# Sums of own rows: 32 adjacency columns stationary in four strips of one bank, then transposed

## The chip, the cores and the metric

The kernel runs on one core of one Trainium2 chip. The metric is the device time of one execution in microseconds (us), and of the kernel before three runs are shown. The engines are TensorE (PE, with its weight loads as PEld), VectorE (DVE), ScalarE (ACT), GpSimd (POOL) and SyncE (SP), which here only issues DMAs. Each works through its own program in order and waits for the others at semaphores.

## The reference

16 graphs of 512 nodes with 128 features go through four layers in a row, each with a residual and a layer norm: a graph convolution with the full adjacency (L0), five small graph convolutions over fixed groups of the first 25 nodes (L1), an attention over the adjacency (L2), and a block of convolutions, a distance matrix and a gated unit (L3).

```python
x = _layernorm(x + _L0_gnn_ref(x, adj, L0_gnn_weight, L0_gnn_bias), axis=-1)
# L0: support = einsum('bni,io->bno', x, weight); out = einsum('bnm,bmo->bno', adj, support) + bias
x = _layernorm(x + _L1_gnn_ref(x, adj, ...), axis=-1)   # written only for nodes 0..24
x = _layernorm(x + _L2_gnn_ref(x, adj, ...), axis=-1)
x = _layernorm(x + _L3_gnn_ref(x, adj, ...), axis=-1)
```

What the change touches is this part of L0: for the graphs 1 to 15 the product of the first 25 rows of the adjacency with x, which is 25 x 512 times 512 x 128 a graph, is needed early, because L1 works on these nodes alone.

## The kernel before

The program has a prologue and a loop. The prologue handles graph 0 up to L2 and, for the graphs 1 to 15 together, L0 and L1 on their 25 first nodes, packed as three tiles (PT = 3) of five graphs (PJ = 5), so that a tile has R = 125 rows. It also loads all weights, transposes them on PE and splits them in a high and a low part. The loop then does one graph a turn, and nothing of the change stands in it.

The 25 rows of each adjacency come in `adjP`, the full x of a tile in `xt[t]` (1280 KB each, loaded by SP in `x_tile`). `transpose_rows(t)` (L851) turns the adjacency rows on PE, ACT's `copy_rows(t)` (L443) puts them in `aPT`. `own_sums(t, graphs)` (L874) multiplies, for each graph and each of four chunks of 128 source nodes, x as the stationary operand (128 columns) by 100 adjacency columns as the moving one, so that the sums come out transposed, with the features on the partitions. Of the 100 columns 25 belong to the graph. ACT's `copy_sums(t)` (L448, L450) picks these into `TTs`, and `own_outputs(t)` (L881) multiplies them by the L0 weight `w0`. A product in float32 is two records in the trace.

There are 15 x 4 = 60 such products. PE has them in pieces between other work in an order that is written by hand: graphs 0 to 3 and then 4 of tile 0 around the first part of graph 0 (L966, L974), one graph of tile 1 ahead of L998, and the other nine graphs behind the transposes `block_rows` (L865). Behind them stand `transpose_weights(-1)` (L917), `own_outputs`, and the second aggregation of graph 0 (L257, L258, L259).

ACT takes its program in order too: `copy_sums(1)`, then `round_weights(-1)` (L479, L480), which copies what L917 wrote, then `copy_sums(2)`, then the exponential L517 and the scaling of the x rows (L520). The input of L517 is a dot product on DVE (L621, released by `dv_f`). DVE continues with L771 and L776 behind L517, and PE's second aggregation waits for L776.

SP loads conv2's weights into the place of `xt[0]` (L376), so it waits until tile 0 has been used (`q_TT` at 1), and behind this in its program stand x and the adjacency of graph 1 (L377, L379). The banks: tile 0's sums use bank 4, tile 1's bank 7, tile 2's bank 0; L998 uses bank 4, and L917's first blocks bank 4 again.

## Time and profile before

| | |
|---|---|
| runs | 588.64, 587.37, 587.83 us; median 587.83 |
| profiled execution | 587.87 us, of which the span is 586.1 us |
| TensorE's granted clock, mean | 0.993 of full |
| busy in the span | PE 568.1, DVE 476.6, ACT 341.3, POOL 120.7 us |
| prologue | from 0 to about 74 us |

The span is the time from the first to the last instruction; what lies around it (1.8 us here) belongs to the execution and not to the program. "Busy" counts the time in which an engine has an instruction under way. A timeline row gives the start, the duration, the engine, the line, the tiles, the shape and the count of like instructions that follow each other, and in brackets the idle time ahead of it with what ended it. The records of PE overlap: the distance from start to start is less than the duration of one.

### The profile page before, as it was taken

The page shows a single profiled execution, that of the slowest core. Times are in us where ns is not written, and L with a number is a line of the kernel's source. Part 1 is how long each engine was busy: PE and PEld are TensorE (multiplying, and loading weights), DVE is VectorE, ACT ScalarE, POOL GpSimd, SP SyncE. Part 2 cuts the span into 40 slices and gives each one's busy share as a digit, 9 for nine tenths or more (in the row PEclk, how much of TensorE's full clock was granted, in tenths as well). Part 3 has the DMA queues.
Part 4 walks back from the last instruction along what each step waited for, and adds up shares of the span by engine and source line. Part 5 has one row for each costly group of instructions (what it writes and reads, how often), then busy time and mean ns, then how long its engine had stood idle before and what let it go on. Part 6 is the DMA issues. An engine that isn't in the chain of part 4 may idle for free.

```text
span 586.1 us, 11733 instructions
## 1 busy us (share of the span) xinstructions
PE 568.1 (97%) x3579; PEld 488.0 (83%) x3579; DVE 476.6 (81%) x1798; ACT 341.3 (58%) x716; POOL 120.7 (21%) x140
## 2 busy tenths in 40 slices
PE   7998999999999999999999999999999999999894
PEld 6896987878979797979888897979797988889684
DVE  4778868888888888888888888888888888888665
ACT  2306646557575656675665757566657566575442
POOL 3310130312213030212131221303021313122110
PEclk9999999999999999999999999999999999999998
DMA  8980032030120303030303012030303030000000
GB/s 187 292 289 2 2 115 82 2 110 1 39 71 1 107 0 108 0 108 0 108 0 95 13 29 79 0 108 0 108 0 108 0 108 1 20 2 19 1 19 18
DMA packets 33300, 34.46 MB, mean 59 GB/s; under 512 B 1663, under 2 KB 22531, under 8 KB 33146
## 3 DMA queue, kind: packets, MB, share of 16 engines
q1 hardware_dynamic: 32986, 34.01, 18.5%
q8 instruction: 13, 0.21, 0.1%
q10 hardware_dynamic: 288, 0.13, 0.1%
q14 instruction: 13, 0.11, 0.1%
HBM read 29.74 MB, written 4.39 MB: 58 GB/s over the span
## 4 chain that ended last, share of the span: by engine, by line
PE 85%; DVE 1%; ACT 0%; issue 0%; POOLq 0%; POOL 0%; DVEq 0%
PE bank L257 14%; PE bank L258 13%; PE bank L259 13%; PE bank L1760 9%; PE pair L257 6%; PE pair L259 6%; PE pair L258 6%; PE bank L1594 4%; PE bank L1605 3%; PE bank L1696 2%; PE pair L1752 2%; PE pair L1684 2%; PE bank L1659 1%; PE bank L1702 1%; PE pair L1711 1%
## 5 line engine op out<-in xcount | busy, mean ns | idle before, releaser
L1133 POOL TENSOR_TENSOR rs<-ve,neg_half 128x4 f32<-128x4 f32 (+1 forms) x60 | 57.2, 953 | 279.1 <-DVE ve L1322 246.3
L257 PE MATMUL bank<-cd_hi,w_hi 128*128 128x256 f32 x272 | 77.5, 285 | 0.0
L258 PE MATMUL bank<-cd_lo,w_hi 128*128 128x256 f32 x272 | 76.7, 282 | 0.0
L259 PE MATMUL bank<-cd_hi,w_lo 128*128 128x256 f32 x272 | 76.5, 281 | 0.0
L1760 PE MATMUL bank<-P,msg 128*128 128x512 f32 x128 | 57.6, 592 | 0.0
L257 PE MATMUL pair<-aT_hi,x_hi 128*128 128x512 f32 x128 | 52.5, 410 | 0.6 <-DVE x_lo L776 0.3
L257 PEld LDWEIGHTS bank<-cd_hi,w_hi 128*128 128x128 f32 x272 | 51.3, 189 | 1.6
L258 PEld LDWEIGHTS bank<-cd_lo,w_hi 128*128 128x128 f32 x272 | 51.4, 189 | 1.4
L259 PEld LDWEIGHTS bank<-cd_hi,w_lo 128*128 128x128 f32 x272 | 51.3, 189 | 0.0
L259 PE MATMUL pair<-aT_hi,x_lo 128*128 128x512 f32 x128 | 50.2, 392 | 0.0
L258 PE MATMUL pair<-aT_lo,x_hi 128*128 128x512 f32 x128 | 50.0, 391 | 0.0
L1354 DVE TENSOR_TENSOR P<-bank,aT 128x512 f32<-128x512 f32 x64 | 41.1, 685 | 9.2 <-ACT bank L1182 9.1
L1341 DVE TENSOR_TENSOR aT_lo<-bank,aT_hi 128x512 fp32r<-128x512 f32 x56 | 38.5, 687 | 8.0 <-ACT aT L1178 8.0
L1176 ACT ACTIVATE aT_hi<-bank 128x512 fp32r<-128x512 f32 x56 | 34.4, 614 | 16.5 <-PE bank L1594 16.5
L1760 PEld LDWEIGHTS bank<-P,msg 128*128 128x128 f32 x128 | 23.1, 190 | 23.0 <-issue 23.0
L257 PE MATMUL bank<-co_hi,w_hi 128*128 128x256 f32 x144 | 41.9, 291 | 0.0
L258 PE MATMUL bank<-co_lo,w_hi 128*128 128x256 f32 x144 | 40.4, 281 | 0.0
L259 PE MATMUL bank<-co_hi,w_lo 128*128 128x256 f32 x144 | 40.4, 280 | 0.0
L1143 POOL TENSOR_TENSOR x<-x_nat,bias 128x512 f32<-128x512 f32 x15 | 19.7, 1316 | 76.6 <-DVE x3T_lo L1429 76.6
L1178 ACT ACTIVATE aT<-bank 128x512 f32<-128x512 f32 x56 | 34.7, 620 | 0.0
L1182 ACT ACTIVATE bank<-bank 128x512 f32<-128x512 f32 x64 | 34.4, 574 | 0.0
L1594 PEld LDWEIGHTS bank<-ident,adj_nat 128*128 128x128 f32 x224 | 26.2, 141 | 9.4 <-issue 7.4
(363 smaller groups left out, 1540.0 us busy)
## 6 DMA issues: line engine op xcount, KB each, us to landing
adj_nat<-in_adj_dram SPq DMA_DIRECT2D x16, 1024.0 KB, 6.1
x_nat<-in_x_dram SPq DMA_DIRECT2D x16, 256.0 KB, 2.9
xt<-in_x_dram SPq DMA_DIRECT2D x3, 1280.0 KB, 11.8
out_dram<-y_out SPq DMA_DIRECT2D x15, 256.0 KB, 2.2
hw<-in_L_gnn_W_dram SPq DMA_DIRECT2D x2, 640.0 KB, 6.9
xt<-in_L_gnn_conv_w_dram SPq DMA_DIRECT2D x1, 1088.0 KB, 9.7
aT<-in_adj_dram SPq DMA_DIRECT2D x5, 96.0 KB
nat_ih<-in_L_gnn_w_ih_dram SPq DMA_DIRECT2D x1, 384.0 KB, 5.4
```

The costliest lines, as they stand in the source:

```text
L257: nc.tensor.matmul(o, lh, rh, start=start, stop=False)
L258: nc.tensor.matmul(o, lh, rl, start=False, stop=False)
L259: return nc.tensor.matmul(o, ll, rh, start=False, stop=stop)
L1133: g.tensor_tensor(rs[i][:, 0:n], ve[i][:, 0:n], neg_half[:, 0:n], ALU.pow).then_inc(po_rs[i], 1)
L1143: g.tensor_tensor(x1[:, :, :], x_nat[1 - par][:, :, :], bc(bias0[:, :], NC), ALU.add).then_inc(po_xb, 1)
L1176: s.activation(aT_hi[:, mc, :], AT_OF[mc][:, :], ACT.Identity)
L1178: s.activation(aT[par][:, mc, :], AT_OF[mc][:, :], ACT.Identity).then_inc(ac_aT[mc], 1)
L1182: s.activation(AT_BANK[mc % 2][:, :], AT_BANK[mc % 2][:, :], ACT.Exp, scale=2.0).then_inc(ac_E[mc], 1)
L1341: v.tensor_tensor(aT_lo[:, mc, :], AT_OF[mc][:, :], f(aT_hi[:, mc, :]), ALU.subtract).then_inc(dv_aTlo[mc], 1)
L1354: v.tensor_tensor(P[:, mc, :], AT_BANK[mc % 2][:, :], aT[par][:, mc, :], ALU.mult).then_inc(dv_P[mc], 1)
L1594: last = t_.transpose(AT_OF[mc][:, ch(c)], adj_nat[par][:, c, ch(mc)], ident[:, :])
L1760: last = t_.matmul(X_BANK[:, :], msg[:, ch(mc)], P[:, mc, :], start=(mc == 0), stop=(mc == NC - 1))
```

## The change

The roles of the operands are exchanged. Now 32 adjacency columns (25 of the graph and 7 that follow) are stationary and 128 features of x move, so a sum comes out with the nodes on the partitions. `own_sums(q)` handles four graphs: graph number `slot` of the four writes the output partitions 32 x slot to 32 x slot + 31 of bank 4 and the columns of group q, and the four graphs take turns within each chunk of source nodes. The fourth group has three graphs. When all four groups are done, ACT copies the bank to `NAT` (`copy_natural`, two instructions; `NAT` is the space of `agg_sb`), PE transposes it in four pieces into bank 0 (`transpose_sums`), and one ACT instruction picks the 25 columns of each graph into `TTs`. `aPT` has three buffers instead of two and 132 columns instead of 125 a chunk, of which POOL fills the last seven once. The conv2 weights now wait for the second group of four, L998 writes bank 7 in place of bank 4, and x3M lies at another address.

```diff
@@ -12,6 +12,8 @@
 PT, PJ = 3, 5
 NT = PT + 1
 R = PJ * NODES
+SLOT = 32
+RW = R - NODES + SLOT
 SUB = 15
 NU = R + (NG - 1) * PJ * SUB
 SPAN = [(g[0][0], g[-1][1]) for g in GROUPS]
...
@@ -140,8 +141,9 @@
         xt = [early(f"xt{i}", [128, PJ, NC, D]) for i in range(PT)]
         nat_c2 = xt[0][:, :, :, :].rearrange("p j c d -> p (j c d)")[:, 0:D * TAPS].rearrange("p (i k) -> p i k", k=TAPS)
         nat_sum = xt[1][:, :, :, :].rearrange("p j c d -> p (j c d)")[:, 0:D * ODD].rearrange("p (i k) -> p i k", k=ODD)
-        aPT = [early(f"aPT{i}", [128, NC, R]) for i in range(2)]
+        aPT = [early(f"aPT{i}", [128, NC, RW]) for i in range(PT)]
         TTs = early("TTs", [128, PT, R])
+        NAT = agg_sb
         xP = early("xP", [128, PT, D])
         x1P = early("x1P", [128, PT, D])
         A5 = early("A5", [128, NT, NG, R])
@@ -152,7 +154,7 @@
         red0 = early("red0", [128, D])
         hw1 = early("hw1", [128, NG, HID])
         hw2 = early("hw2", [128, NG, 2, D])
-        hT = [aPT[h][:, 0:PT, :] for h in range(2)]
+        hT = [aPT[h][:, :, :].rearrange("p c r -> p (c r)")[:, 0:PT * R].rearrange("p (t r) -> p t r", t=PT) for h in range(2)]
         S2 = early("S2", [128, PT, D])
         R2 = early("R2", [128, PT, D])
...
+        NAT_BANK, TT_BANK = bank[4], bank[0]
         LATE = [[], [2, 3], [4, 5], [6, 7], [8]]
         LATE_AT = [[2], [3], [], [], []]
 
...
                 sp.dma_start(nat_hh[:, :, :], a["L3_gnn_w_hh"].rearrange("(g o) k -> o g k", g=3)).then_inc(q_wt, 16)
-                sp.wait_ge(q_TT, 1)
+                sp.wait_ge(q_sums, 2)
...
                 last.then_inc(q_zero, 1)
+                for t in range(PT):
+                    last = g.memset(aPT[t][:, :, R:RW], 0.0)
+                last.then_inc(q_pad, 1)
                 pool.wait_ge(q_ident, 1)
...
@@ -438,17 +444,19 @@
                                   ).then_inc(q_cst, 16)
                 def copy_rows(t):
                     act.wait_ge(q_aP, t + 1)
-                    if t > 1:
-                        act.wait_ge(q_TT, t - 1)
-                    s.activation(aPT[t % 2][:, :, :], bank[4 if t == 0 else 7][:, 0:NC * R].rearrange(
+                    s.activation(aPT[t][:, :, 0:R], bank[4 if t == 0 else 7][:, 0:NC * R].rearrange(
                         "p (c r) -> p c r", c=NC), ACT.Identity).then_inc(q_aPT, 1)
 
-                def copy_sums(t):
-                    act.wait_ge(q_TT, t + 1)
-                    s.activation(TTs[:, t, 0:R - NODES].rearrange("p (j n) -> p j n", n=NODES),
-                                 TT_BANK[t][:, 0:(PJ - 1) * R].rearrange("p (j n) -> p j n", n=R)[:, :, 0:NODES], ACT.Identity)
-                    s.activation(TTs[:, t, R - NODES:R], TT_BANK[t][:, (PJ - 1) * R - NODES:(PJ - 1) * R], ACT.Identity
-                                 ).then_inc(q_TTs, 1)
+                def copy_natural():
+                    act.wait_ge(q_sums, 4)
+                    s.activation(NAT[:, 0:3 * 128], NAT_BANK[:, 0:3 * 128], ACT.Identity)
+                    s.activation(NAT[0:3 * SLOT, 3 * 128:N], NAT_BANK[0:3 * SLOT, 3 * 128:N], ACT.Identity).then_inc(q_sumsb, 1)
+
+                def copy_sums():
+                    act.wait_ge(q_TT, 1)
+                    s.activation(TTs[:, :, :].rearrange("p t (j n) -> p (t j) n", n=NODES),
+                                 TT_BANK[:, 0:SLOT * (B - 1)].rearrange("p (g n) -> p g n", n=SLOT)[:, :, 0:NODES],
+                                 ACT.Identity).then_inc(q_TTs, 1)
 
                 def copy_u(t):
                     act.wait_ge(q_U, t + 1)
...
                 s.activation(U0[:, 0:NG, :], bank[6][:, 0:R].rearrange("p (g n) -> p g n", g=NG), ACT.Identity).then_inc(q_U0s, 1)
-                copy_sums(0)
                 copy_rows(2)
                 act.wait_ge(q_fuse, 2)
                 s.activation(fw[:, 2, :], fw[:, 1, :], ACT.Exp).then_inc(q_fe, 1)
@@ -510,9 +517,9 @@
                 act.wait_ge(q_S0, 1)
                 s.activation(S0[0:NODES, 0:4, :], bank[5][0:NODES, :].rearrange("p (g d) -> p g d", g=4), ACT.Identity)
                 s.activation(S0[0:NODES, 4, :], bank[6][0:NODES, 0:D], ACT.Identity).then_inc(q_S0s, 1)
-                copy_sums(1)
+                copy_natural()
                 round_weights(-1)
-                copy_sums(2)
+                copy_sums()
                 act.wait_ge(dv_f, 1)
                 s.activation(pef[:, 1, :], ef[:, 1, :], ACT.Exp, bias=c12[:, 1:2]).then_inc(ac_pf, 1)
                 hold(act, ac_pf, 1)
...
-                    o = bank[4][0:NODES, ch(gi)] if gi < 4 else bank[6][0:NODES, 0:D]
+                    o = bank[7][0:NODES, ch(gi)] if gi < 4 else bank[6][0:NODES, 0:D]
...
@@ -865,19 +872,30 @@
                             last = t_.transpose(o, A5[0:R, t, gi, :], ident[0:R, 0:R])
                     last.then_inc(q_BT, 1)
 
-                def own_sums(t, graphs):
-                    pe.wait_ge(q_aPT, t + 1)
-                    pe.wait_ge(q_xr[t], 16)
-                    for j in graphs:
-                        for mc in range(NC):
-                            lo = 0 if j < PJ - 1 else NODES
-                            last = t_.matmul(TT_BANK[t][:, 100 * j:100 * (j + 1)], xt[t][:, j, mc, :],
-                                             aPT[t % 2][:, mc, lo:lo + 100], start=(mc == 0), stop=(mc == NC - 1))
-                    if PJ - 1 in graphs:
-                        last.then_inc(q_TT, 1)
+                def own_sums(q):
+                    graphs = range(4 * q, min(4 * q + 4, B - 1))
+                    pe.wait_ge(q_pad, 1)
+                    pe.wait_ge(q_aPT, graphs[-1] // PJ + 1)
+                    for t in range(graphs[0] // PJ, graphs[-1] // PJ + 1):
+                        pe.wait_ge(q_xr[t], 16)
+                    for mc in range(NC):
+                        for slot, k in enumerate(graphs):
+                            t, j = k // PJ, k % PJ
+                            last = t_.matmul(NAT_BANK[SLOT * slot:SLOT * (slot + 1), ch(q)],
+                                             aPT[t][:, mc, NODES * j:NODES * j + SLOT], xt[t][:, j, mc, :],
+                                             start=(mc == 0), stop=(mc == NC - 1))
+                    last.then_inc(q_sums, 1)
+
+                def transpose_sums():
+                    pe.wait_ge(q_nT, 2)
+                    for q in range(4):
+                        pe.wait_ge(q_sumsb, 1)
+                        rows_ = SLOT * min(4, B - 1 - 4 * q)
+                        last = t_.transpose(TT_BANK[:, 128 * q:128 * q + rows_], NAT[0:rows_, ch(q)], ident[0:rows_, 0:rows_])
+                    last.then_inc(q_TT, 1)
 
                 def own_outputs(t):
-                    pe.wait_ge(q_TTs, t + 1)
+                    pe.wait_ge(q_TTs, 1)
                     return t_.matmul(bank[7][0:R, ch(t)], TTs[:, t, :], w0[:, :], start=True, stop=True)
 
                 def hidden(gi):
@@ -953,19 +971,16 @@
                     last = t_.matmul(AG_BANK[:, ch(c)], agg_sb[:, ch(c)], w0[:, :], start=True, stop=True)
                 last.then_inc(pe_out0, 1)
                 block_rows(0)
-                own_sums(0, (0,))
                 pe.wait_ge(q_row, 16 * 14)
                 pe.wait_ge(q_aPT, 2)
                 t_.matmul(bank[7][:, 0:D], vrows[0:NROWS, :], ident[0:NROWS, :], start=True, stop=True).then_inc(q_cols, 1)
-                own_sums(0, (1,))
                 pe.wait_ge(q_colsb, 1)
                 transpose_rows(2)
-                own_sums(0, (2, 3))
+                own_sums(0)
                 pe.wait_ge(dv_x1, 1)
                 pe.wait_ge(q_nT, 1)
                 t_.matmul(bank[6][:, 0:R].rearrange("p (g n) -> p g n", g=NG), x1[0:NODES, 0, :], nadjT[0:NODES, 0, :, 0:NODES],
                           start=True, stop=True).then_inc(q_U0, 1)
-                own_sums(0, (4,))
                 pe.wait_ge(q_zero, 2)
                 pe.wait_ge(q_U0s, 1)
                 pe.wait_ge(q_h1, 16)
@@ -990,23 +1005,22 @@
                         last = t_.matmul(o, hT0[:, 2 * gi + h, :], hw2[:, gi, h, :], start=(h == 0), stop=(h == 1))
                 last.then_inc(q_S0, 1)
                 pe.wait_ge(q_c12, 1)
-                own_sums(1, (0,))
                 pe.wait_ge(q_S0s, 1)
-                pe.wait_ge(q_TTs, 1)
                 for gi in range(NG):
-                    o = bank[4][0:NODES, ch(gi)] if gi < 4 else bank[6][0:NODES, 0:D]
+                    o = bank[7][0:NODES, ch(gi)] if gi < 4 else bank[6][0:NODES, 0:D]
                     last = t_.matmul(o, nadjT[0:NODES, 0, gi, 0:NODES], S0[0:NODES, gi, :], start=True, stop=True)
                 last.then_inc(q_o0, 1)
                 block_rows(1)
+                own_sums(1)
                 block_rows(2)
                 block_rows(3)
-                own_sums(1, range(1, PJ))
-                pe.wait_ge(q_nT, 2)
-                own_sums(2, range(PJ))
-                pe.wait_ge(q_own, 5)
+                own_sums(2)
+                own_sums(3)
+                pe.wait_ge(q_sumsb, 1)
                 pe.wait_ge(q_sc1, 1)
                 transpose_weights(-1)
-                pe.wait_ge(q_TTs, 2)
+                transpose_sums()
+                pe.wait_ge(q_own, 5)
                 for t in range(PT):
                     last = own_outputs(t)
                 last.then_inc(q_o, 1)
```

PE, early in the prologue, before. L874 are the products of own rows, L851 the transposes of tile 2's adjacency rows, L966 and L974 the small convolutions of graph 0:

```order
L959 MATMUL bank<-ident,vrows 128x128
L874 MATMUL bank<-aPT,xt 128x100 x4
L851 MATMUL bank<-ident,aT 128x125 x4
L874 MATMUL bank<-aPT,xt 128x100 x8
L966 MATMUL pair<-nadjT,x 128x125
L874 MATMUL bank<-aPT,xt 128x100 x4
```

The same place after, where L884 are the products, L858 the transposes of adjacency rows, L976 the former L959, L982 the former L966:

```order
L976 MATMUL bank<-ident,vrows 128x128
L858 MATMUL bank<-ident,aT 128x125 x4
L884 MATMUL bank<-xt,aPT 32x128 x16
L982 MATMUL pair<-nadjT,x 128x125
L989 MATMUL bank<-U,hw 128x100 x10
```

The 20 products of tile 0 in four pieces have become 16 in one piece, ahead of L982.

PE from the second layer of graph 0 (L990) to the own outputs (L881), before:

```order
L990 MATMUL pair<-hw,hT 25x128 x10
L874 MATMUL bank<-aPT,xt 128x100 x4
L998 MATMUL bank<-prod,nadjT 25x128 x4
L998 MATMUL pair<-prod,nadjT 25x128
L865 MATMUL bank<-ident,A 125x125 x15
L874 MATMUL bank<-aPT,xt 128x100 x36
L917 MATMUL bank<-ident,nat_w 128x128
L917 MATMUL bank<-ident,nat_wm 128x128
L917 MATMUL bank<-ident,nat_ws 128x128
L881 MATMUL bank<-w,TTs 125x128 x3
```

The same place after; L1005 is the former L990, L1011 the former L998, L872 the former L865, L935 the former L917, L894 the new transposes and L899 the own outputs:

```order
L1011 MATMUL bank<-prod,nadjT 25x128 x4
L1011 MATMUL pair<-prod,nadjT 25x128
L872 MATMUL bank<-ident,A 125x125 x5
L884 MATMUL bank<-xt,aPT 32x128 x16
L872 MATMUL bank<-ident,A 125x125 x10
L884 MATMUL bank<-xt,aPT 32x128 x28
L935 MATMUL bank<-ident,nat_w 128x128
L935 MATMUL bank<-ident,nat_wm 128x128
L935 MATMUL bank<-ident,nat_ws 128x128
L894 MATMUL bank<-ident,agg_sb 128x128 x3
L894 MATMUL bank<-ident,agg_sb 128x96
L899 MATMUL bank<-w,TTs 125x128 x3
```

No product stands ahead of L1011 any more, 16 stand between the transposes L872, 28 behind them, and four transposes are new behind the weights.

ACT from the copy of v (L508) to the exponential L517, before:

```order
L508 ACTIVATE v<-bank 128x256
L511 ACTIVATE prod<-pair 25x512
L512 ACTIVATE prod<-pair 25x128
L448 ACTIVATE TTs<-bank 128x100
L450 ACTIVATE TTs<-bank 128x25
L479 ACTIVATE plainT<-bank 128x3
L480 ACTIVATE plainT<-bank 128x2x128
L448 ACTIVATE TTs<-bank 128x100
L450 ACTIVATE TTs<-bank 128x25
L517 ACTIVATE pef<-ef,c 128x4
```

The same place after, where L515 is the former L508, L452 and L453 the new copy of the bank, L457 the new pick, and L524 the former L517:

```order
L515 ACTIVATE v<-bank 128x256
L518 ACTIVATE prod<-pair 25x512
L519 ACTIVATE prod<-pair 25x128
L452 ACTIVATE agg_sb<-bank 128x384
L453 ACTIVATE agg_sb<-bank 96x128
L487 ACTIVATE plainT<-bank 128x3
L488 ACTIVATE plainT<-bank 128x2x128
L457 ACTIVATE TTs<-bank 128x375
L524 ACTIVATE pef<-ef,c 128x4
```

Of the copies L448 and L450 none is left, and ahead of L487 stands the copy of the whole bank.

## Rows read from the trace of the kernel before

**Rows 1.** Page, busy time, share and instructions of each engine, whole span.
```profile
PE 568.1 (97%) x3579; PEld 488.0 (83%) x3579; DVE 476.6 (81%) x1798; ACT 341.3 (58%) x716; POOL 120.7 (21%) x140
```

**Rows 2.** Waits, 17 to 47 us: who waited, for whom, us in total, times, longest.
```profile
ACT TTs L448 <- PE bank L874: 8.3, 2, 7.5
```

**Rows 3.** Timeline of PE, 31 to 49 us: start, us, line, tiles, shapes, idle before.
```profile
31.43 1.11 PE L874 MATMUL bank<-aPT,xt 128*128 128x100 f32 x8 [0.54 <-DMA xt<-in_x_dram]
32.47 1.05 PE L998 MATMUL bank<-prod,nadjT 25*25 25x128 f32 x8
...
33.67 1.90 PE L865 MATMUL bank<-ident,A 125*125 125x125 f32 x15
35.41 8.18 PE L874 MATMUL bank<-aPT,xt 128*128 128x100 f32 x72
43.42 0.27 PE L917 MATMUL bank<-ident,nat_w 128*128 128x128 f32 x1
...
45.90 0.47 PE L257 MATMUL pair<-aT_hi,x_hi 128*128 128x512 f32 x1 [0.30 <-DVE x_lo L776]
...
48.75 0.60 PE L924 MATMUL bank<-ident,adj_nat 128*128 128x128 f32 x4
```

**Rows 4.** Timeline of ACT, 31 to 45 us.
```profile
31.42 0.25 ACT L512 ACTIVATE prod<-pair 25x128 f32<-25x128 f32 x1
...
43.95 0.17 ACT L479 ACTIVATE plainT<-bank 128x3 f32<-128x3 f32 x1 [4.46 <-PE bank L917]
...
44.49 0.32 ACT L517 ACTIVATE pef<-ef,c 128x4 f32<-128x4 f32 x1
```

**Rows 5.** Timeline of DVE, 41 to 45 us.
```profile
41.48 0.08 DVE L621 DVE_READ_ACCUMULATOR2_ANT ef<- 128x1 f32 x1
44.91 0.17 DVE L771 CAST x_hi<-pef 128x4 fp32r<-128x4 f32 x1 [3.35 <-ACT pef L517]
```

**Rows 6.** Timeline of PE, 20 to 29 us.
```profile
20.08 0.48 PE L959 MATMUL bank<-ident,vrows 28*128 28x128 f32 x2
...
21.47 0.65 PE L851 MATMUL bank<-ident,aT 125*128 125x125 f32 x4
...
23.81 0.48 PE L966 MATMUL pair<-nadjT,x 25*128 25x125 f32 x2
...
25.20 2.40 PE L974 MATMUL bank<-U,hw 128*128 128x100 f32 x20
...
28.55 2.34 PE L990 MATMUL pair<-hw,hT 128*25 128x128 f32 x20 [0.48 <-issue]
```

**Rows 7.** Timeline of PE, one place of the loop, at 84.75 us.
```profile
84.75 0.39 PE L1711 MATMUL pair<-ident_r,G 128*64 128x128 f32 x4
```

**Rows 8.** Timeline of ACT at 58.63 us.
```profile
58.63 0.49 ACT L471 ACTIVATE S<-bank 125x384 f32<-125x384 f32 x1 [0.23 <-PE bank L903]
```

**Rows 9.** Timeline of SP's DMA issues, 19 to 34 us.
```profile
19.06 0.43 SPq L365 DMA_DIRECT2D hw<-in_L_gnn_W_dram  x1
19.53 4.96 SPq L343 DMA_DIRECT2D xt<-in_x_dram  x2
...
31.44 1.52 SPq L376 DMA_DIRECT2D xt<-in_L_gnn_conv_w_dram  x1
...
33.84 1.41 SPq L379 DMA_DIRECT2D adj_nat<-in_adj_dram  x1
```

**Rows 10.** Lines L365, L343 and L379: first and last issue, issue to landing.
```profile
DMA to landing us min/median/max: 8.9/8.9/8.9
...
L343 SPq DMA_DIRECT2D xt<-in_x_dram x3: 390/1375/3547, 10.9 to 20.9; - x3
...
DMA to landing us min/median/max: 7.5/11.8/14.3
...
DMA to landing us min/median/max: 10.7/10.7/10.7
```

**Rows 11.** DMA issues, whole span: name, count, size, median us to landing.
```profile
adj_nat<-in_adj_dram SPq DMA_DIRECT2D x16, 1024.0 KB, 6.1
```

9 lines of the change are left out of this document (4 added, 5 removed).

## Prediction

> **What bounds the kernel now.** I read the page first: TensorE (PE) is busy for 97% of the span [rows 1], so a microsecond that leaves PE's path in the prologue should leave the end. The change touches only the prologue (before about 74 us), so I took the list of waits for the stretch 17 to 47 us: ScalarE (ACT) waits 8.3 us for the products of L874, the sums of own rows, [rows 2], and VectorE (DVE) then waits 3.35 us for ACT's L517 [rows 5]. The reader is to see one chain there. PE's timeline [rows 3] has 72 records of L874 from 35.41 for 8.18 us with no idle time in them, and only then the weight transposes of L917 at 43.42. ACT takes its work in the order written, so L479 (43.95) and L517 (44.49) stand behind PE's L917 [rows 4], although the input of L517, the last dot product on DVE, was done at 41.48 + 0.08 = 41.56 [rows 5]. From L517 go DVE's L771 at 44.91 [rows 5] and the second aggregation, L257 at 45.90, 1.41 us behind L517, which ends where L924 begins, at 48.75 [rows 3]. So the sums of own rows are the bound from 35 to 43 us. What stands in line behind them: the dot product (41.56, at most 44.49 - 41.56 = 2.9 us to be had unless it too moves), then the weights, x rows and adjacency that SP loads.
>
> **Products.** Before there are 60 products, each written as two records (120 in all), with 128 stationary and 100 moving columns. 72 records in 8.18 us, the last one 0.27 long: (8.18 - 0.27) / 71 = 0.111 us a record, 0.223 a product [rows 3]. After there are again 60 products of two records, with 32 stationary and 128 moving columns. The nearest row is L990, 25 stationary and 128 moving columns: (2.34 - 0.27) / 19 = 0.109 a record, 0.218 a product [rows 6]. So narrower weights alone bring 2%. The whole gain hangs on whether products for different strips of 32 output partitions run beside one another; no row of before has this (L990 and L998 always write the first strip). Bounds of a product:
> - no overlap: 0.218;
> - full overlap of the four: eight records in 0.218, 0.055 a product. L1711 issues weight load and matmul pairs (0.39 - 0.22) / 3 = 0.057 apart [rows 7], so pairs of that pace are possible, and 0.055 to 0.114 stands for full overlap;
> - the value I take, 0.14: the two records of a product go to the same strip and stay 0.109 apart; only the next product's first record may start beside the second record of this one, some 0.03 behind it (half of the pace of L1711, my estimate).
>
> The Trainium skill (TensorEngine Tiling (Array Packing), Overview) gives column tiling at 32 columns or fewer "Up to 4×", and its Key Properties say that tiles load weights and multiply in parallel; by that alone a product would cost 0.055 and the time would be that of rival B. TensorE: Matmul & The Clock Gate (Part 3, Packing small matmuls) says that matmuls start and end strictly in program order; with the two records of one product on one strip that order gives 0.14 instead. No row of before shows either.
>
> **Early part.** The program is moved too, as the order shows: 20 products of tile 0 that stood between L959 and L974 become 16 behind L851. L851 starts at 21.47 now, behind L874's second piece; after, it waits for L959 (20.08) and ACT's copy of it, some 0.8 later, so it starts near 20.85 and ends near 21.4 [rows 6]. 16 products of 0.14 end at 23.6, L966 starts there (23.81 before); its ACT copy takes until about 24.4 as now, and no product stands between it and L974, which starts at 24.45 instead of 25.20. That gives DVE's chain 0.75 us, so the dot product is done at 40.8. L990 gains less: its weights hw2 land at 19.06 + 8.9 = 27.96 [rows 9, 10], so it starts at 28.05 instead of 28.55, and L998 starts when ACT's L512 is done, at 31.42 + 0.25 - 0.5 = 31.17 [rows 4], say 31.25, instead of 32.47, since no product of tile 1 (landing 19.53 + 11.8 = 31.33 [rows 9, 10]) stands ahead of it.
>
> **Middle part.** From L998 at 31.25: ten records of 0.109 to 32.35; five transposes of L865 at 0.11, to 32.9 (DVE's operands for them come 0.75 earlier too); 16 products, 2.24, to 35.15; ten transposes, 1.1, to 36.25; 28 products, 3.9, to 40.2 (tile 2 is issued at 20.9 and has landed at 20.9 + 14.3 = 35.2 [rows 10], no wait). I add 0.1 for the changes between the shapes: the products end at 40.3 where they ended at 43.42. That is 3.1 us less.
>
> **What is added behind them.** Before, L517 came 44.49 - 43.42 = 1.07 us behind the products. After, the first step is a copy: PE's last record takes 0.27 to end, ACT copies 128x384 (the like of L471, 0.49, the next instruction starting 0.1 earlier [rows 8]) and 96x128 (0.25, as L512 [rows 4]), which ends 0.95 behind the products. PE's three transposes of L917 wait for this, because they write the same bank; they take 0.22 + 0.27, ACT's L479 starts at 1.45 and L480 ends at 1.85; the four transposes of sums are done by then, the copy of 375 columns takes 0.48 with 0.1 overlapped, and L517 starts 2.25 behind the products: 40.3 + 2.25 = 42.55. The chain behind the products is 1.2 us longer than before. Behind the waiting copies on ACT stand L517 and the scaling of x rows, behind the waiting transposes on PE the own outputs and the second aggregation. 42.55 is above the dot product's 40.8, so ACT still decides. The own outputs (six records, 0.65) and L917's four (0.45) fill PE from 42.7 to 43.8; the aggregation starts at 42.55 + 1.41 = 43.96 instead of 45.90. **The gain is 1.9 us.**
>
> **Moved transfers.** SP issued conv2's weights at 31.44 and the second adjacency at 33.84 [rows 9]. The first now waits for the second group of products (35.15), because it overwrites tile 0, so both go some 3.8 us later, the adjacency at 37.65. In the steady part an adjacency lands 6.1 us behind its issue, here in the crowd it took 10.7 [rows 10, 11]: 43.75 to 48.35, and it is wanted at 43.96 + 2.85 = 46.8 (2.85 is 48.75 - 45.90 [rows 3]). The crowd (tile 2 and what follows it) is gone by 38, so I take 45 and no cost; if the cover is gone, up to 1.5 us. The three fills on GpSimd, the bank exchange 4 to 7 for L998 and the new place of x3M cost nothing: GpSimd is idle until a DMA lands then, bank 7 is free, and x3M is written only in the loop. The rest of the prologue hangs on the aggregation and moves with it.
>
> Sum against the profiled execution: span 586.1 - 1.9 = 584.2, with 1.8 around it 586.0; that run (587.87) is 0.04 above the median of the runs, so **585.9 us**.
>
> **Rivals.**
> - B, full overlap. Products at 0.06: the early group ends at 22.4, DVE's chain gains 1.9 (dot product at 39.7), the products end near 36.9 (tile 2 lands at 35.2, 28 products take 1.7), and L517 starts at the dot product, 39.75: 4.7 us less. The aggregation would end at 45.90 - 4.7 + 2.85 = 44.05, before an adjacency that can hardly land ahead of 44.7: 0.7 given back, 583.9. For it: four separate strips. Against: the pairs of records on one strip.
> - C, no overlap, the other side. One mechanism: each product waits for the one ahead as in L990, at 0.218. The early group ends at 24.9 and L966 behind it, DVE's chain and L990 are 0.55 late, L998 starts at 32.3, and 10 records, 15 transposes and 44 products (9.6) end at 44.65; the chain behind is 1.2 longer, so L517 comes at 46.9, 2.4 late: 590.3. It decides from about 0.18 a product on: there 44 x 0.043 more uses up the 1.9. For it: L990 shows that a narrow stationary operand gives nothing by itself [rows 6]. Against: here four strips are named in turn.
> - D, the second adjacency becomes the bound: overlap as forecast, but landing at 48.3 instead of 45: 1.5 lost, 587.4. For it: 10.7 us now. Against: fewer bytes are ahead of it.
>
> **Chances.** Forecast 0.50 (its own range 584.6 to 587.0, from 0.11 to 0.165 a product), B 0.17, C 0.23, D 0.10. The likeliest gives 585.9. The range 583.4 to 589.8 leaves out the far half of C and a small part of B. No change means within 0.2%, 1.2 us, about what a measurement of this kernel can tell: faster has the forecast but 0.05 of it and B, 0.62; same has 0.05 and most of D, 0.14; slower has C and a rest, 0.24.
>
> **What would show it.** In the profile after: the 120 product records, and their spacing (pairs 0.11 apart with a short gap to the next: forecast; all near 0.03: B; all 0.11: C); last product near 40.3; L517's successor near 42.55 with ACT waiting first for the products, then for L917; the aggregation near 43.96; no wait of PE for adjacency at 46.8. I am wrong if strips share the array less than the pairs allow, if switching between shapes costs more than 0.1 in all, or if a transfer is late.

## The result

The changed kernel takes 584.18 us (median of 17 runs, 580.93 to 587.54) against 587.37 us for the kernel before on the same chips (17 runs, 585.7 to 590.47): a ratio of 0.9937, 95% interval 0.9917 to 0.9957. By the ratio that is 3.7 us less, by the two medians 3.2. Forecast were 585.9 us and a gain of 1.9. The time lies in the stated range and the direction was right; the gain is about twice the forecast one, and nearest to the time was rival B (583.9). The profiled execution has a span of 582.4 us, 3.7 less than the 586.1 of before.

Each run also has TensorE's mean granted clock over its span, and the two kernels differ in it. For the kernel before it was 0.990 to 0.997 in the 71 runs made beside the experiments; in the 24 of the changed kernel (17 here, 7 of after_again) it was 0.980 to 0.996, and in 8 of them below 0.990. At an equal mean clock the kernels lie further apart: at 0.993 the mean is 587.3 us over 20 runs of before and 583.3 over 7 of the changed kernel, at 0.996 586.2 over 21 and 581.9 over 2. From this I estimate that the change is worth about 4 us at equal clock and that a lower clock gives some of it back; the runs are of several chips, so the figure is rough.

The page of the profile after: the first line answers to [rows 1], with 7.8 us less on PE; the second is the granted clock in 40 slices of 14.6 us, in tenths.

```profile
PE 560.3 (96%) x3583; PEld 479.4 (82%) x3583; DVE 476.7 (82%) x1798; ACT 341.6 (59%) x713; POOL 120.8 (21%) x143
...
PEclk9989999999999999999999999999999999999998
```

PE's timeline after, which answers to [rows 3, 6]. L884 are the products; L858, L976, L982, L989, L1011, L872, L935 and L942 the former L851, L959, L966, L974, L998, L865, L917 and L924:

```profile
20.16 0.48 PE L976 MATMUL bank<-ident,vrows 28*128 28x128 f32 x2
20.93 0.74 PE L858 MATMUL bank<-ident,aT 125*128 125x125 f32 x4 [0.28 <-ACT cols L506]
21.60 1.08 PE L884 MATMUL bank<-xt,aPT 128*32 128x128 f32 x32
23.39 0.48 PE L982 MATMUL pair<-nadjT,x 25*128 25x125 f32 x2 [0.71 <-DVE x L682]
24.29 2.44 PE L989 MATMUL bank<-U,hw 128*128 128x100 f32 x20 [0.41 <-issue]
...
31.02 1.03 PE L1011 MATMUL bank<-prod,nadjT 25*25 25x128 f32 x8 [0.93 <-ACT prod L519]
...
32.19 1.30 PE L872 MATMUL bank<-ident,A 125*125 125x125 f32 x5
33.43 1.93 PE L884 MATMUL bank<-xt,aPT 128*32 128x128 f32 x32
35.29 1.56 PE L872 MATMUL bank<-ident,A 125*125 125x125 f32 x10
36.78 1.95 PE L884 MATMUL bank<-xt,aPT 128*32 128x128 f32 x56
39.49 0.33 PE L935 MATMUL bank<-ident,nat_w 128*128 128x128 f32 x1 [0.76 <-ACT agg_sb L453]
...
39.88 0.57 PE L894 MATMUL bank<-ident,agg_sb 128*128 128x128 f32 x4
...
42.29 0.47 PE L260 MATMUL pair<-aT_hi,x_hi 128*128 128x512 f32 x1
...
45.13 0.60 PE L942 MATMUL bank<-ident,adj_nat 128*128 128x128 f32 x4
```

The reader is to see three things. The 32 records of the first group take 1.08 us: (1.08 - 0.27) / 31 = 0.026 a record, 0.052 a product, where before a product took 0.223. The last 56 took (1.95 - 0.27) / 55 = 0.031, 0.061 a product; 24 of them belong to the group of three graphs, which fills three strips only. The 32 records at 33.43 take 1.93, and the five transposes ahead of them 1.30 where they should take 4 x 0.116 + 0.27 = 0.74 ((1.90 - 0.27) / 14 = 0.116 from the 15 of [rows 3]). And the last products end at 36.78 + 1.95 = 38.73 instead of at 43.59, while L989 starts at 24.29 instead of at 25.20.

ACT and DVE after, which answer to [rows 4, 5]: L452 and L453 copy the bank, L487 is the former L479, L457 picks the sums, L524 is the former L517; L628 is the end of the dot product, L778 the former L771.

```profile
38.79 0.49 ACT L452 ACTIVATE agg_sb<-bank 128x384 f32<-128x384 f32 x1 [7.92 <-PE bank L884]
39.17 0.26 ACT L453 ACTIVATE agg_sb<-bank 96x128 f32<-96x128 f32 x1
40.08 0.17 ACT L487 ACTIVATE plainT<-bank 128x3 f32<-128x3 f32 x1 [0.64 <-PE bank L935]
...
40.49 0.48 ACT L457 ACTIVATE TTs<-bank 128x375 f32<-128x375 f32 x1
40.90 0.30 ACT L524 ACTIVATE pef<-ef,c 128x4 f32<-128x4 f32 x1
```

```profile
40.78 0.08 DVE L628 DVE_READ_ACCUMULATOR2_ANT ef<- 128x1 f32 x1
41.29 0.17 DVE L778 CAST x_hi<-pef 128x4 fp32r<-128x4 f32 x1 [0.43 <-ACT pef L524]
```

L524 starts at 40.90, 3.59 us before the 44.49 of the kernel before, and the second aggregation at 42.29, 3.61 us before its 45.90; the span is 3.7 shorter. So in these two profiles the gain arose ahead of L524 and nothing of it was lost behind. The dot product ended at 40.78 + 0.08 = 40.86: DVE's wait for L524 fell from 3.35 to 0.43 us [rows 5]. Both inputs of L524 come at the same time here, the copy chain (L457 ends at 40.97, and the next instruction of ACT starts some 0.1 ahead of that end) and the dot product.

The granted clock in six microseconds of the prologue: stretch, its length, busy time and instructions by engine, the clock, DMA share and GB/s.

```profile
30.00:36.00 6.00, 5.07 (x52) 4.00 (x52) 5.93 (x23) 0.74 (x2) 0.00 (x0) 0.72 0.91 259
```

Half speed (1.2 GHz in place of 2.4) for about 3.4 of the six microseconds gives 0.72. That is what stretched L872 and the second group. There is another such stretch, from 11.9 to 15.3 us, in the first aggregation of graph 0, ahead of everything that was moved; I come back to it below.

### The profile page after: what moved, and what is told of

Its sections match the earlier page's. It is cut to its first block, busy times and chain, and to the rows that moved or that the text cites. A ratio compares the mean times of both kernels' runs of the same rounds, so it can differ in the third digit from the quotient of the medians.

```text
span 582.4 us, 11740 instructions
## 1 busy us (share of the span) xinstructions
PE 560.3 (96%) x3583; PEld 479.4 (82%) x3583; DVE 476.7 (82%) x1798; ACT 341.6 (59%) x713; POOL 120.8 (21%) x143
## 4 chain that ended last, share of the span: by engine, by line
PE 85%; DVE 1%; ACT 0%; issue 0%; POOLq 0%; POOL 0%; DVEq 0%
PE bank L260 14%; PE bank L262 14%; PE bank L261 13%; PE bank L1774 9%; PE pair L260 6%; PE pair L262 6%; PE pair L261 6%; PE bank L1608 4%; PE bank L1619 3%; PE bank L1710 2%; PE pair L1766 2%; PE pair L1698 2%; PE bank L1673 1%; PE bank L1716 1%; PE pair L1725 1%
```

## The experiments

| kernel | ratio to before, interval | median | products of the last groups | dot product ready | L524 starts | mean clock, 16 to 30 us | profiled run |
|---|---|---|---|---|---|---|---|
| before (profile) | | 587.37 | 8.18 | 41.56 | 44.49 | 1.00 | 587.87 |
| before, 2nd profile | | | 8.18 | 41.36 | 43.81 | 1.00 | 586.03 |
| after (profile) | 0.9937, 0.9917 to 0.9957 | 584.18 | 1.95 | 40.86 | 40.90 | 1.00 | 584.18 |
| after_again | 0.9951, 0.9923 to 0.9979 | 584.01 | 1.95 | 40.99 | 41.03 | 0.88 | 583.14 |
| slot_major | 0.9981, 0.9963 to 0.9999 | 586.37 | 3.86 | 41.81 | 45.23 | 0.88 | 587.61 |
| more_late | 0.9969, 0.9947 to 0.9990 | 585.42 | 3.69 | 42.23 | 44.10 | 0.76 | 587.42 |
| more_early | 0.9961, 0.9941 to 0.9981 | 585.21 | 1.95 | 41.54 | 41.58 | 1.00 | 584.85 |
| two_strips | one run | 584.68 | 2.48 | 41.34 | 41.38 | 1.00 | 584.68 |
| own_first | 0.9957, 0.9939 to 0.9974 | 584.45 | 1.99 | 41.56 | 41.66 | 0.76 | 584.08 |
| adj_first | 0.9950, 0.9929 to 0.9971 | 584.25 | 1.97 | 45.37 | 45.41 | 0.65 | 587.82 |
| pool_scale | 0.9958, 0.9936 to 0.9980 | 584.63 | 1.95 | 44.00 | 44.04 | 0.76 | 588.59 |
| warm | 0.9943, 0.9923 to 0.9962 | 582.21 | 1.95 | 39.56 | 39.60 | 1.00 | 581.70 |
| warm_best | 0.9934, 0.9921 to 0.9948 | 583.04 | 1.95 | 40.86 | 40.90 | 0.88 | 582.96 |

Times in us; the five columns on the right are of each kernel's one profiled execution, L524 under its name in the changed kernel (L517 before). The kernel before had medians of 587.07 beside after_again to more_early, 587.04 beside two_strips and own_first to pool_scale, and 586.68 beside the warm ones.

One reading goes for the whole table: the profiled run less the start of L524 is 542.1 to 543.4 us in twelve of the thirteen rows (pool_scale 544.6), while L524 itself moves by 5.8 us. So what tells the executions apart is almost all ahead of L524. And a profile need not be like the median of its kernel: those of adj_first, pool_scale and more_late were 3.6, 4.0 and 2.0 us above theirs, so that their L524 columns show a late execution, and where profile and median differ the verdict rests on the median.

**slot_major: the same products, strip after strip.**

```diff
-                    for mc in range(NC):
-                        for slot, k in enumerate(graphs):
+                    for slot, k in enumerate(graphs):
+                        for mc in range(NC):
```

> The order of the products is changed, graph by graph, so that the four chunks of one graph (one strip) follow each other and no two neighbours are in different strips except at the change of graph. All else as in the changed kernel. Theory 1 (the strips run beside one another, 0.027 us a record instead of 0.109): the records go back to 0.109 each, the products of the last two groups (56 records) take 6 us instead of 1.9, the last product ends near 43.5 and the time is 3 to 6 us above the changed kernel, so at or above the kernel before. Theory 2 (32 stationary columns are cheap by themselves, whatever the strip): same time as the changed kernel, within 1 us.

PE's timeline, the three groups of products, and ACT's exponential:

```profile
20.64 3.94 PE L884 MATMUL bank<-xt,aPT 128*32 128x128 f32 x32
...
33.99 4.05 PE L884 MATMUL bank<-xt,aPT 128*32 128x128 f32 x32
...
39.25 3.86 PE L884 MATMUL bank<-xt,aPT 128*32 128x128 f32 x56
```

```profile
45.23 0.29 ACT L524 ACTIVATE pef<-ef,c 128x4 f32<-128x4 f32 x1
```

The first two groups took longer for their 32 records than the third for its 56 because the clock was at half speed from 20.4 to 23.9 and from 34.1 to 37.5; only the third group is to be read for the pace. Nothing but the order was changed, and the median rose by 2.4 us (586.37 against 584.01 for after_again on the same chip; the two intervals just overlap, 0.9963 to 0.9979). L524 came 3.4 us behind the dot product, of which half speed in the second group explains about 1.7, an estimate from the 3.4 us at half speed. So the products bind again, and the records show that strips side by side are the source of their pace, not narrow weights: theory 1. But its sizes were off, in time (3 to 6 us) and in pace: 56 records took 3.86, (3.86 - 0.27) / 55 = 0.065 a record and not 0.109. The first half microsecond of this group and the next, in a windows view (instructions of PE and PEld in the second and third column):

```profile
39.24:39.70 0.47, 0.47 (x5) 0.46 (x5) 0.33 (x2) 0.00 (x0) 0.00 (x0) 1.00 0.55 94
39.70:40.17 0.47, 0.47 (x10) 0.47 (x9) 0.36 (x3) 0.00 (x0) 0.00 (x0) 1.00 0.42 150
```

Five records in the first 0.47 us, about 0.109 apart, ten in view in the next: I read this as the second strip's records starting while about half of the eight of the first strip still wait. Then twice as many run at once although the program gives them strip by strip. No record names its strip; the reading rests on the first five, which belong to one strip and stand 0.109 apart.

**two_strips: two strips in turns, then the other two.**

```diff
-                    for mc in range(NC):
-                        for slot, k in enumerate(graphs):
+                    for pair_ in (0, 2):
+                        for mc, slot in [(m, sl) for m in range(NC) for sl in (pair_, pair_ + 1) if sl < len(graphs)]:
```

> Within a group of four graphs the products of strips 0 and 1 take turns and are finished before those of strips 2 and 3. Theory 1 (a strip takes one record per 0.109 us, and records of different strips run beside one another if they are near in the program): two records run at a time, 32 records take about 1.9 us instead of 1.08, and the last 56 about 3.1 instead of 1.95, somewhat less where the next pair of strips starts beside the end of the first. Theory 2 (records are simply issued every 0.027 us on average, whatever the strip): 1.08 and 1.95 us as in the changed kernel.

```profile
22.18 1.54 PE L885 MATMUL bank<-xt,aPT 128*32 128x128 f32 x32
...
33.45 1.54 PE L885 MATMUL bank<-xt,aPT 128*32 128x128 f32 x32
...
36.20 2.48 PE L885 MATMUL bank<-xt,aPT 128*32 128x128 f32 x56
```

1.54 us for 32 records and 2.48 for 56, between the two theories: (1.54 - 0.27) / 31 = 0.041 a record, with four strips in turns 0.026, with one after the other 0.065. The order sets the pace by how many strips are near one another, and since two at a time would give 0.109 / 2 = 0.055 a record, more than two ran beside each other here too. L524 at 41.38 waited for the dot product, so in this single execution the products, at 0.082 each, no longer bound.

**more_late and more_early: the same extra work at two places.**

`signal` only keeps the repeated groups from raising the semaphore more than once; that part of the edit is left out here.

```diff
-                own_sums(2)
-                own_sums(3)
+                for signal in (False, True):
+                    own_sums(2, signal)
+                    own_sums(3, signal)
```

```diff
-                own_sums(0)
+                for signal in (False, False, True):
+                    own_sums(0, signal)
```

> The products of the third and fourth group are computed twice (56 records more, about 1.5 us of TensorE at full clock), behind the transposes of the adjacency blocks. Theory 1 (the bound is now the dot product on VectorE, ready at 40.84 where the exponential on ScalarE starts at 40.90, and TensorE has about 1.5 us to spare at full clock): the time rises by less than 1 us. Theory 2 (the products with the longer chain behind them still bound): the time rises by the full 1.5 us, and the exponential starts 1.5 us behind the dot product.

> The products of the first group are computed three times (64 records more, about 1.75 us of TensorE at full clock), ahead of the small convolution of graph 0 on which VectorE's chain hangs. Theory 1 (VectorE's chain, which starts from there, is the bound): the time rises by 1 to 1.75 us, more than in the run with the late products doubled, and the dot product is ready as much later. Theory 2 (only what stands at the late place counts): no change, within 0.5 us.

> The changed kernel once more, on the same chip as the others of this call: 0.993 to 0.995 of the kernel before. Theory on the clock: the granted clock fell to half for 3.4 us at 32 us in the profile of the changed kernel and not in that of before; if this belongs to the changed kernel, it is there again in this profile near that place; if it is chance, it is absent or elsewhere.

The repeated products in both:

```profile
38.27 3.69 PE L884 MATMUL bank<-xt,aPT 128*32 128x128 f32 x112
```

```profile
21.16 2.83 PE L884 MATMUL bank<-xt,aPT 128*32 128x128 f32 x96
...
46.37 0.66 PE L943 MATMUL bank<-ident,adj_nat 128*128 128x128 f32 x4 [0.39 <-DMA adj_nat<-in_adj_dram]
```

The extra work is 1.74 us (56 more records, 3.69 - 1.95) and 1.75 us (64 more, 2.83 - 1.08) in the profiles, the time rose by 1.4 and 1.2 us against after_again, and the intervals overlap, so the times don't tell the theories apart. The profiles say more. In more_late L524 came 1.87 behind the dot product: the spare time that theory 1 claimed was used up. The extra 1.74 is more than the 1.36 to spare in after_again (below), and half speed (21.0 to 27.9 and 34.7 to 38.1) had delayed PE as well. In more_early L524 followed the dot product at once (41.54, 41.58) although 64 records more stood ahead. Its last row also shows PE waiting 0.39 us for the second adjacency, which no other profile has. In after_again, where the clock was full behind 24.1 us, ACT waited 1.36 us for the dot product:

```profile
41.03 0.30 ACT L524 ACTIVATE pef<-ef,c 128x4 f32<-128x4 f32 x1 [1.36 <-DVE ef L628]
```

So with the clock full in this part VectorE's chain is the bound with 1.36 us to the next, and with a stretch at half speed in 30 to 36 us, as in the first profile, the two meet. On the clock the expectation of after_again was right for chance: there was a stretch of 3.4 us, but from 20.7 to 24.1 and not near 32.

**own_first and adj_first.**

```diff
                 block_rows(0)
+                own_sums(0)
                 pe.wait_ge(q_row, 16 * 14)
...
-                own_sums(0)
```

```diff
-                sp.wait_ge(q_sums, 2)
-                sp.dma_start(nat_c2, a["L3_gnn_conv2_w"]).then_inc(q_wc2, 16)
-                sp.dma_start(x_nat[1][:, :, :], x_v[1]).then_inc(x_in[1], 16)
                 sp.wait_ge(q_A5, 2)
                 sp.dma_start(adj_nat[1][:, :, :], adj_v[1]).then_inc(adj_in[1], 16)
+                sp.dma_start(x_nat[1][:, :, :], x_v[1]).then_inc(x_in[1], 16)
+                sp.wait_ge(q_sums, 2)
+                sp.dma_start(nat_c2, a["L3_gnn_conv2_w"]).then_inc(q_wc2, 16)
```

> The first group of products stands ahead of the wait for the vector rows (L976) instead of behind the transposes of tile 2, so that it fills the 1.4 us in which TensorE waits there. Theory 1 (VectorE's chain from the small convolution of graph 0 to the dot product is the bound): that convolution, at 23.4 now with its input ready at 21.4, starts 1 to 1.9 us earlier, the dot product is ready 1 to 1.7 us earlier, and the time falls by 0.5 to 1.5 us against the changed kernel, less what the second adjacency gives back. Theory 2 (the products and the copy chain behind them bound): no change.

> SP issues x and adjacency of graph 1 ahead of the wait for the second group and of conv2's weights, so the adjacency is issued near 31.7 instead of 36.2. Theory 1 (the adjacency, landing at 44.3 to 44.7 for a use at 45.1 to 45.3, costs nothing or a few tenths): landing near 42, no change beyond 0.5 us. Theory 2 (the later landing costs time in some executions): 0.5 to 1 us faster than the changed kernel and a smaller spread.

Issue to landing of the second adjacency, in the changed kernel (issued at 36.29) and in adj_first (issued at 30.97), and the small convolution L989 in own_first and adj_first:

```profile
DMA to landing us min/median/max: 8.4/8.4/8.4
```

```profile
DMA to landing us min/median/max: 9.4/9.4/9.4
```

```profile
21.84 0.78 PE L982 MATMUL pair<-nadjT,x 25*128 25x125 f32 x2
23.04 4.53 PE L989 MATMUL bank<-U,hw 128*128 128x100 f32 x20 [0.41 <-issue]
```

```profile
26.06 4.51 PE L989 MATMUL bank<-U,hw 128*128 128x100 f32 x20 [0.41 <-issue]
```

The adjacency landed at 36.29 + 8.4 = 44.69 for a use at 45.13, and in adj_first at 30.97 + 9.4 = 40.4; the medians (584.25, and 584.45 for own_first beside it) and intervals are alike, so its late issue costs nothing that shows (theory 1 of adj_first, rival D out). The room is small, 0.44 us. own_first did start the small convolution earlier (L982 at 21.84 with its input at 21.4), but L989 behind it took 4.53 us instead of 2.44: the clock was at half speed from 20.6 to 27.4, and no gain was left: the dot product was ready at 41.56, 0.6 later than in after_again and not 1 to 1.7 earlier as theory 1 has it. In the profile of adj_first the stretch was 10.2 us long, L989 took 4.51, and DVE waited 5.4 us for it; that is how a profiled run comes to 587.82 with a median of 584.25. This is a cause that none of my theories had.

**pool_scale: one of three scalings on GpSimd.**

```diff
-                for t in range(1, NT):
+                for t in range(1, NT - 1):
...
+                pool.wait_ge(q_dgi, 2)
+                g.tensor_tensor(A5[0:R, 3], A5[0:R, 3], spread(deg[0:R, 3, NG * 3:NG * 4], R), ALU.mult).then_inc(q_B3, 1)
...
-                    pe.wait_ge(q_B, t + 1)
+                    pe.wait_ge(q_B3 if t == 3 else q_B, 1 if t == 3 else t + 1)
```

> One of the three scalings of the masked adjacency (L726, 0.75 us each on VectorE) runs on the idle GpSimd instead. Theory 1 (VectorE's chain bounds): the dot product is ready 0.7 us earlier, the time falls by 0.3 to 0.7 us. Theory 2 (it does not bound): no change; if the third scaling comes late on GpSimd, TensorE's transposes of the blocks and all products behind them are late by that much.

DVE's scalings (L728) and first dot product (L630), then the shortest, the median and the longest of the two scalings in ns, and GpSimd's work beside them:

```profile
33.30 2.57 DVE L728 TENSOR_TENSOR A<-A,deg 125x625 f32<-125x625 f32 x2
35.79 1.09 DVE L630 CUSTOM_DVE_ANT_0 prod<-x,v 128x128 f32<-128x128 f32 x1
```

```profile
L728 DVE TENSOR_TENSOR A<-A,deg x2: 810/1324/1839, 33.3 to 34.0; 125x625 f32<-125x625 f32 x2
```

```profile
33.34 1.85 POOL L428 TENSOR_TENSOR A<-A,deg 125x625 f32<-125x625 f32 x1 [6.20 <-DVE deg L575]
35.49 1.23 POOL L430 TENSOR_TENSOR xP<-xP,bias 125x384 f32<-125x384 f32 x1 [0.29 <-DMA xP<-in_x_dram]
```

No gain: the median is 584.63, beside 584.45 and 584.25 on the same chip. Two scalings took 2.57 us where three take 2.25 in the changed kernel, but not in equal parts: the first, begun just ahead of GpSimd's L428, took its usual 0.81, the second, begun at 34.02 with L428 under way, 1.84. The first dot product, begun with L430 under way, took 1.09 in place of 0.29. VectorE lost 0.3 + 0.8 us by what should have saved 0.75. In the profile of adj_first, too, the first dot product (at 37.11) took 1.09, beside the addition on GpSimd (L428 there, 36.45 to 38.05), while the scaling begun just ahead of that addition took its usual 0.80. In all three cases the slow instruction ended behind GpSimd's, the dot products by 0.15 us and the scaling by 0.67, which is 0.14 less than each takes alone: as if it had stood still almost until then. Why is not shown. In the profile of the changed kernel DVE's scalings and dot products and this GpSimd work missed one another. That L524 came as late as 44.04 here is in good part the clock: at half speed from 22.0 to 28.9, the small convolution took 4.56 us.

**warm, warm_best and before_again: the clock.**

```diff
-                for i in range(32):
+                for i in range(40):
                     t_.transpose(bank[7][:, 0:D], ident[:, :], ident[:, :])
...
+                pe.wait_ge(dv_y1, 1)
+                for i in range(12):
+                    t_.transpose(bank[5][:, 0:D], ident[:, :], ident[:, :])
                 pe.wait_ge(q_row, 16 * 14)
...
+                pe.wait_ge(ac_aT[0], 1)
+                for i in range(8):
+                    t_.transpose(bank[0][:, 0:D], ident[:, :], ident[:, :])
                 pe.wait_ge(q_S0s, 1)
```

warm_best has 4 transposes in place of the 12, with the edits of own_first and adj_first.

> The changed kernel with transposes of the identity that nobody reads put where TensorE waits: 8 more at the start, 12 ahead of the wait for the vector rows (from 18.4 to 19.7), 8 ahead of the wait for ACT's S0 (from 30.3 to 31.2). Theory of the clock (TensorE's idle stretches in the prologue, which the old products filled, let its granted clock fall to 1.2 GHz for 3.4 to 10.2 us from about 20 on, and this delays VectorE's chain by up to 2 us): no stretch at half clock between 16 and 50 us in the profile, the small convolution L989 takes 2.4 us and not 4.5, and the median falls by 1 to 2 us against the changed kernel. Rival (the falls come by chance, whatever TensorE does there): a fall as in the other runs, and the same time within 0.5 us.

> The same idea with the first group of products ahead of the wait for the vector rows and only 4 transposes behind it, 8 more at the start, 8 ahead of S0, and the adjacency of graph 1 issued ahead of conv2's weights. Theory of the clock with VectorE's chain as bound: clock full from 16 to 50 us, the dot product ready near 39.5, time 2 to 3 us below the changed kernel, 0.988 to 0.992 of the kernel before. Rival (products and copies bound, clock by chance): within 0.7 us of the changed kernel.

> The kernel before once more, for a second profile. Theory of the clock: no stretch at half clock between 16 and 50 us, where its products of 128 stationary columns stand in what are gaps in the changed kernel. Rival (chance): a fall of 3.4 us or more near 20 us or 33 us here too.

The stretch from 16 to 30 us in before_again, after_again, adj_first and warm, one row each:

```profile
16.00:30.00 14.00, 13.51 (x114) 12.47 (x114) 10.65 (x66) 5.27 (x14) 5.62 (x4) 1.00 0.90 289
```

```profile
16.00:30.00 14.00, 11.42 (x105) 9.49 (x104) 10.61 (x66) 4.44 (x12) 5.12 (x4) 0.88 0.93 298
```

```profile
16.00:30.00 14.00, 11.39 (x86) 9.62 (x84) 8.57 (x60) 4.55 (x11) 5.62 (x4) 0.65 0.96 298
```

```profile
16.00:30.00 14.00, 12.81 (x128) 10.99 (x128) 12.02 (x69) 5.33 (x14) 5.12 (x4) 1.00 0.85 279
```

The products, the small convolution and the exponential in warm (L985 is the former L982, L992 the former L989):

```profile
21.22 1.08 PE L884 MATMUL bank<-xt,aPT 128*32 128x128 f32 x32
22.23 0.48 PE L985 MATMUL pair<-nadjT,x 25*128 25x125 f32 x2
23.12 2.45 PE L992 MATMUL bank<-U,hw 128*128 128x100 f32 x20 [0.41 <-ACT U L510]
```

```profile
39.60 0.30 ACT L524 ACTIVATE pef<-ef,c 128x4 f32<-128x4 f32 x1 [1.36 <-DVE ef L628]
```

All nine profiles of kernels with the new products and without fillers have a stretch of 3.4 to 10.2 us at half speed that begins somewhere between 11 and 46 us; neither of the two profiles of the kernel before has one there, nor has warm; warm_best has one of 3.4 us at 23.3, so its expectation (clock full, dot product near 39.5) failed. Two things weaken the count. In two_strips the only stretch, and in the changed kernel's first profile one of two, begins at 11.7 and 11.9, ahead of the first place where PE's program differs from the one before, so that it can't come from what the old products filled. And such stretches occur elsewhere too, with either kernel: the profile of before has one of 3.4 us at 554, as five of the others have at 551 to 555, and all thirteen end with one of about 6 us or more. What leaves little to chance is the clock of all the runs: below 0.990 in 8 of 24 runs of the changed kernel, in 31 of 72 of its six variants without fillers that ran twelve times each, and in none of 71 of the one before. Each stretch of 3.4 us lowers the mean by 1.7 / 582 = 0.003, and over the 17 runs of the result 0.003 less clock goes with 1.1 us more time (a fitted line).

Why the changed kernel has more of them is argued, not shown. In the stretch from 16 to 30 us PE was busy 13.51 of 14 us in before_again and 11.42 in after_again: the old products filled the waits for the vector rows (from 18.4 to 19.75 us) and for S0. But own_first, too, put products into the first of these waits, and fell to half speed at 20.6 all the same.

The fillers are best compared with after_again, where the first aggregation ended at the same time (L858 starts at 15.31 there and at 15.33 in warm). The dot product was ready at 39.56 in place of 40.99, 1.4 us earlier, with the clock at 1.00 instead of 0.88. In time warm can't be told from the changed kernel: its ratio, 0.9943 with the interval 0.9923 to 0.9962, contains 0.9937. Its seven runs fall in two parts, and the clock goes with them: four at 581.7 to 582.2 us have 0.996, three at 584.0 to 585.6 have 0.987 to 0.990. So the fillers did not keep the clock up in every run. With either set of fillers the clock was 0.987 to 0.996, on average 0.993 over 13 runs, where the changed kernel has 0.990 over 24 on other chips; that is a hint, and what the fillers are worth stays open. No version here is shown to beat the changed kernel; warm_best has the lowest upper end (0.9948).

## Why the prediction was right in sign and half in size

- **The bound before** (ACT's L517 behind 72 records, with the dot product 2.9 us ahead of it) was read rightly: the change took L524 to the dot product and the span followed to 0.1 us. The forecast had the products still bind (42.55 against 40.8); in fact both were ready at the same time in this profile and the products 1.36 us ahead in after_again, so that what they gained beyond the dot product was worth nothing.
- **The cost of a product**, the term on which everything hung, failed: 0.14 was taken, 0.052 measured in groups of four graphs and 0.061 over the last 28 products. The step that failed is "the two records of a product go to the same strip and stay 0.109 apart; only the next product's first record may start beside the second record". A windows view of 0.11 us from the start of the first group shows what takes its place (PE records, one of them the end of the transposes, and PEld records in the second and third column):

```profile
21.59:21.70 0.11, 0.11 (x5) 0.10 (x8) 0.11 (x3) 0.11 (x1) 0.00 (x0) 1.00 0.44 140
```

Four product records and eight weight loads stand within it. The trace has these four within 0.02 us (21.599 to 21.619), the next four from 21.733 and then four more every 0.109 us. Since records of one strip stand 0.109 apart in slot_major, I read the four as the first records of the four strips and the next four as the second ones, although each product's second record follows its first in the program; no record names its strip. Eight records in 0.22 us is the full overlap that was given as the lower bound. Two sentences of the Trainium skill were weighed. The "Up to 4×" of the Trainium skill's TensorEngine Tiling (Array Packing), Overview, agrees: the 96 records of more_early took (2.83 - 0.27) / 95 = 0.027 each, a quarter of the 0.109 of L990. The strict program order of matmul starts in the Trainium skill's TensorE: Matmul & The Clock Gate, Part 3, does not agree with slot_major, if the records are read as above: those of a second strip start ahead of waiting ones of the first. The measurement decides, and I had built the 0.14 on the wrong one of the two.
- **Early part.** L998 was forecast at 31.25 and started, as L1011, at 31.02. Forecast L989 at 24.45 and the dot product at 40.8; measured 24.29 and 40.86. This is partly luck: the first aggregation ended 1.35 us later in this execution (L858 at 17.25, L851 at 15.90 before), 0.14 of it because the adjacency landed later (L955 at 11.04, L937 at 10.90 before) and the other 1.2 in the stretch at half speed from 11.9 to 15.3. VectorE's x was late by it, and L982 waited 0.71 us for that and not for the products. So the chain itself was faster by more, as rival B had it, and the clock gave some back; that two errors met at 40.8 was chance.
- **Products' end.** Forecast 40.3, counted as the 43.42 before; measured in that count 38.46, with (1.30 - 0.81) + (1.93 - 1.08) + (1.56 - 1.35) = 1.55 us lost to half speed (L872, L884 and L872 at 32.19, 33.43 and 35.29 against 0.81, 1.08 and 1.35 in after_again). The forecast had no term for the clock.
- **Chain behind the products.** Forecast 2.25 from the products' end to L524; measured from 38.46 (38.73 less the 0.27 of the last record) to 40.90, 2.44, with the dot product at 40.86 as the other bound. Right.
- **Transfers.** Forecast landing 45, no cost; measured 44.69 and none; rival D did not come. Right.
- **Rivals.** C (no overlap) was refuted, and even the worst order, slot_major, has 0.13 a product. B came true in its mechanism; it had L524 at 39.75, near the value of warm (39.60). The changed kernel's profile came to this part 1.9 us later than warm (L858 at 17.25 against 15.33), 0.7 of it by the later adjacency and 1.2 at half speed from 11.9 to 15.3, and its dot product was ready 1.3 later.

## What to carry to other kernels

Products with few stationary columns gain next to nothing alone (0.218 us with 25 columns against 0.223 with 128), but with 32 columns and given to four strips of output partitions in turns they ran four at a time: 0.052 us each, at the price of a transpose and two copies. Order them so that neighbours are in different strips. Then look at the granted clock, in the profile by stretch and in all runs by their mean: a kernel with less work on TensorE may run more of it at half speed (below 0.990 in 8 of 24 runs here, in none of 71 before), and a time compared without the clock then mixes the two. Why it does was not settled here.

## What was not expected of the hardware

- Records given strip after strip run beside one another: 0.065 us a record, 0.041 with two strips in turns, 0.026 with four, where one strip alone has 0.109.
- The granted clock fell to 1.2 GHz for 3.4 to 10.2 us in the prologue of all nine profiles with the new products and without fillers. PE was busy 79 to 90% of the time from 16 to 30 us in these, 96 to 97% in the two profiles of before. Where such a stretch covered L989 it took 4.5 us in place of 2.4. Two of the stretches began at 11.7 and 11.9, behind a wait of 2.15 and of 3.19 us for the first adjacency; before_again waited 2.14 us there and had none.
- A VectorE instruction begun while GpSimd had a tensor instruction under way was slow: 1.84 in place of 0.80 us for a scaling of 125x625, 1.09 in place of 0.29 for a dot product of 128x128. GpSimd's addition over 125x384 took 1.23 and 1.60 us there in place of 1.00.
